# A graph layer on one core: keys packed once for all edges, a reordered preparation, and the test for further passes moved

## The chip, the core and the metric

One core of a Trainium2 chip runs the whole program. The time is the device time of one execution, in microseconds. An execution of the kernel before took 666.23 us (median of 3 runs, 665.59 to 668.93). The engines are TensorE (PE in the rows; PEld is its weight load), VectorE (DVE), ScalarE (ACT), GpSimd (POOL) and SyncE (SP, which only issues DMAs here). An engine works its instructions off in program order, and waits on semaphores hold up all that is behind them.

## The reference

6250 nodes of 96 values, 206250 edges sorted by their target `dst`, and a small perceptron:

```python
h = maximum(layernorm(x), 0)
m = h[src] + edge_attr                       # 206250 x 96
aggr = segment_sum(m, dst, num_segments=6250)
hidden = relu(aggr @ W1 + b1)                # 96 -> 192
out = x + (1 + eps) * h + hidden @ W2 + b2   # 192 -> 96
```

## The kernel before

The nodes are cut into 49 blocks of 128. Since `dst` is sorted, the edges of a block lie together. For each block the kernel builds, without any gather, an adjacency count: for every node of the block how often each of the 6250 sources points at it. Aggregation is then `adj` (counts) times `h`, plus the sums of the edge rows.

Preparation, once. `dst` is loaded as 127 rows of 1632 (`D`), every 32nd of its values is taken as a sample, and one-hots of the samples and 51 matmuls give the histogram from which the start row of each node in the sorted list follows (`hist`, `total`, `cnt`, `row`). GpSimd subtracts neighbours in `D` (line 369) and VectorE takes the minimum (`falls`), to see whether `dst` is sorted. `row` gives the place of each node's window of 128 edges (`row_i`) and, spread by matmul, the edge row at which each group of 32 nodes starts (`e_tab`), which SyncE reads for its loads. Beside it VectorE and ScalarE make `h` (mean, centre, square, variance, root, scale; lines 499 to 516) and split it in two fp16 parts `hl` (lines 518 to 522). Copies of `src` and `dst` with a padded tail are written to DRAM, since the windows are fetched from there.

The loop over blocks b = 0 to 48 (and one more turn of TensorE and ScalarE). All engines work on different blocks at the same time, ordered by semaphores:

- GpSimd, once for two blocks (a pair): two indirect DMAs fetch the windows of 128 edges of 128 target pairs from the padded `src` and `dst`; ten vector instructions of 128 columns compute a low key (source modulo 128) and a high key (source block and which of the two targets) from them (`keys`, lines 373 to 391); then it adds the bias `b2` to the pair's part of `x_sb`.
- TensorE turns a pair's keys (`turn_keys`, line 814). ScalarE copies the turned keys out of PSUM, each value twice, once per block (`next_keys`, 256 columns, behind its octet copy 6).
- VectorE compares: `hot` (which of 32 nodes an edge belongs to, from the block's 4 x 10 x 128 edge ids), and in four chunks the one-hots `z` (source block) and `lo_hot` (source modulo 128) (line 494).
- TensorE multiplies `lo_hot` and `z` in eight octets of 8 slots, into one of two PSUM banks in turn; ScalarE copies each octet to `adj` (line 722). TensorE sums the edge rows (80 passes of 32 columns, behind octet 3), one block later the slots `adj` x `hl` (49 matmuls, line 832, behind octet 1), then turns the sums (line 837, behind octet 4), and runs the perceptron. ScalarE takes the low half of the sums, the turned sums and the relu from PSUM; VectorE joins (line 618) and adds the result to `x_sb` (line 625).
- SyncE loads the edge rows and ids of each block in four groups (`load`, lines 291 to 296), into a ring of 4 buffers (`TURN`), and stores block b - 8 behind the load of block b. The residual `x + (1 + eps) h` (line 589) stands on VectorE between block 0 and block 1. `h` lives in buffers 2 and 3 of the edge ring, so loads 2 and 3 wait for the residual.

The end. A window may be too short for unusual inputs; the number of passes that is needed is computed on VectorE (`passes_needed`, behind the last block) and each engine tests it: if it is over 1 (it is 1 here) a general loop would do all again. Before the test, all five engines wait for all stores (`all_stored`).

Of the kernel before, what the change touches and what calls it, by code (L numbers as in the profile page):

```python
# [12 lines left out]
P = 128  # L13
# [10 lines left out]
TURN = 4  # L24
SCALE = 4096.0
EDGES_AFTER = 3
ROUND = 12582912.0


def build(nc, x, src, dst, edge, w1, b1, w2, b2, eps, out):  # L30
# [3 lines left out]
    NT = -(-N // P)  # L34
    NLAST = N - (NT - 1) * P
    ZW = NT * TILE_NODES
    SAMPLES = -(-E // STEP)
    PAIRS = -(-NT // 2)
    GE = P * GT
    ELAST = E - GE  # L40
    GCOLS = PAIRS * 2 * GROUPS
    TURNS = NT // TURN
    assert NT == TURNS * TURN + 1 and ZW % 2 == 0

# [4 lines left out]
    assert 0 < DREST < DW and DW % STEP == 0  # L49

    EVEN = E // 16 * 16
    PADDED = (SAMPLES + 4) * STEP
    PAD = PADDED - EVEN
# [3 lines left out]
    FAR = 32767  # L57

    with ExitStack() as ctx:
# [8 lines left out]

        src_pad = nc.dram_tensor("src_padded", [PADDED], I32).ap()
        dst_pad = nc.dram_tensor("dst_padded", [PADDED], I32).ap()  # L70
        src_rows = src_pad.rearrange("(r k) -> r k", k=STEP)
        dst_rows = dst_pad.rearrange("(r k) -> r k", k=STEP)
# [7 lines left out]
        dst_sb = [sb(f"dst{k}", [P, GROUPS, GT], I32) for k in range(TURN)]  # L80
        z_home = sb("z", [P, CHUNKS, CHUNK, ZW], F16)
# [3 lines left out]
        hot = [sb(f"hot{k}", [P, GROUPS * GT, GROUP]) for k in range(2)]  # L85
        rel = [sb(f"rel{k}", [P, GROUPS, GT]) for k in range(2)]
        key2 = [sb(f"key{k}", [P, 2, TPB, 2], F16) for k in range(2)]

        win_src = [sb(f"win_src{k}", [P, P], I32) for k in range(2)]
        win_dst = [sb(f"win_dst{k}", [P, P], I32) for k in range(2)]  # L90
        k_lo = sb("k_lo", [P, P])
        k_hi = sb("k_hi", [P, P])
        k_a = sb("k_a", [P, P])
        k_src = sb("k_src", [P, P])
        k_w = sb("k_w", [P, P])
        keyT = [sb(f"keyT{k}", [P, 2, P]) for k in range(2)]
# [15 lines left out]
        total = sb("total", [PAIRS, P])  # L112
# [8 lines left out]
        picked = sb("picked", [P, 2, PAIRS, 2 * GROUPS])  # L121
# [25 lines left out]
        tail_ids = sb("tail_ids", [1, 2, PAD], I32)  # L147
# [10 lines left out]
        ob = [sb(f"ob{k}", [P, C]) for k in range(TURN)]  # L158
# [790 lines left out]
```

## Time and profile before

| | before |
|---|---|
| median of 3 runs | 666.23 us |
| the profiled execution's own time | 665.97 us |
| its span, first to last instruction | 664.1 us |
| VectorE busy | 586.3 us, 88% |
| TensorE busy | 536.5 us, 81% |
| GpSimd busy | 473.9 us, 71% |
| ScalarE busy | 374.3 us, 56% |
| DMA moved | 109.72 MB, 165 GB/s on average |

Busy times are sums over the whole span. No engine is busy throughout, and the chain from one block to the next runs over several engines; so the table alone doesn't tell what sets the time. The granted clock of TensorE is 1.00 of its 2.4 GHz from 50 to 640 us.

### The profile page before, as it was taken

Reading aid. Unit: us, or ns where it says so; the run is one execution under the profiler, and the core shown is the slowest. Engines: PE = TensorE matmul, PEld = TensorE weight load, DVE = VectorE, ACT = ScalarE, POOL = GpSimd, SP = SyncE. Lnnn points to the kernel's source line nnn. Section 1 sums busy time; section 2 is a strip of 40 time slices with the busy share of each in tenths; the row PEclk is TensorE's granted clock in tenths of the full one; section 3 lists DMA queues with packets and bytes.
Section 4 is the critical chain, followed back from the end, with each engine's and each line's share of the span. In section 5 each row is a group of like instructions: output and inputs, shape, how many; then the busy total and the mean of one; then the engine's idle time right before and its main releaser. Section 6 shows DMA issues by size and latency. Waiting matters only on the chain. (4 is left out here: it accounts for less than half of the span.)

```text
span 664.1 us, 24207 instructions
## 1 busy us (share of the span) xinstructions
PE 536.5 (81%) x10016; PEld 492.7 (74%) x10016; DVE 586.3 (88%) x649; ACT 374.3 (56%) x645; POOL 473.9 (71%) x393
## 2 busy tenths in 40 slices
PE   0301598999989999898998989999899998989982
PEld 0301487888878888788888878888788887888881
DVE  6998699999999999999999999999999999999830
ACT  2221356567565665756667565665656657566650
POOL 4199999999977977977887797797779777730000
PEclk9999999999999999999999999999999999999997
DMA  8271785656656565565646656465564665644000
GB/s 244 66 223 38 239 259 154 189 170 193 192 165 201 152 205 182 162 195 174 206 159 184 188 172 204 156 189 191 164 198 158 197 187 171 200 139 125 6 5 9
DMA packets 67888, 109.72 MB, mean 165 GB/s; under 512 B 40093, under 2 KB 41727, under 8 KB 67742
## 3 DMA queue, kind: packets, MB, share of 16 engines
q1 hardware_dynamic: 66174, 104.84, 51.9%
q0 software_dynamic: 1600, 3.28, 1.6%
q8 instruction: 81, 1.33, 0.8%
q14 instruction: 33, 0.27, 0.1%
HBM read 105.69 MB, written 4.05 MB: 165 GB/s over the span
## 5 line engine op out<-in xcount | busy, mean ns | idle before, releaser
L722 ACT ACTIVATE adj<-oct_ps 128x784 f16<-128x784 f32 x392 | 316.8, 872 | 79.1 <-PE oct_ps L820 73.8
L494 DVE TENSOR_TENSOR lo_hot<-iota_z,key 128x2048 f16<-128x2048 f16 x196 | 263.9, 1346 | 0.0
L820 PE MATMUL oct_ps<-z,lo_hot 128*128 128x98 f16 x3136 | 201.1, 208 | 48.7 <-ACT adj L722 39.6
L494 DVE TENSOR_TENSOR z<-iota_z,key 128x1568 f16<-128x1568 f16 x196 | 198.5, 1013 | 36.2 <-PE oct_ps L820 35.5
L820 PEld LDWEIGHTS oct_ps<-z,lo_hot 128*128 128x128 f16 x3136 | 162.3, 98 | 78.7 <-issue 54.8
L832 PE MATMUL agg_ps<-hl,adj 128*128 128x192 f16 x2401 | 206.0, 246 | 0.0
L832 PEld LDWEIGHTS agg_ps<-hl,adj 128*128 128x128 f16 x2401 | 196.9, 98 | 0.2 <-ACT adj L722 0.2
L728 ACT ACTIVATE low<-agg_ps 128x96 f32<-128x96 f32 x49 | 12.3, 252 | 157.3 <-PE agg_ps L832 157.3
L826 PE MATMUL agg_ps<-edges,hot 128*32 128x96 f32 x3920 | 92.6, 250 | 0.0
L826 PEld LDWEIGHTS agg_ps<-edges,hot 128*32 128x32 f32 x3920 | 81.9, 111 | 4.1
L598 DVE TENSOR_TENSOR hot<-iota_w,rel 128x1280 f32<-128x1280 f32 x49 | 73.6, 1502 | 1.7
L375 POOL TENSOR_SCALAR k_hi<-win_src 128x128 f32<-128x128 int32 x25 | 18.4, 738 | 65.4 <-PE key_ps L814 64.9
L394 POOL DMA_INDIRECT win_src<-src_padded,row_i x25 | 43.6, 1743 | 18.3 <-DVE row_i L549 14.3
L396 POOL DMA_INDIRECT win_dst<-dst_padded,row_i x25 | 39.2, 1567 | 7.6 <-issue 7.6
L846 PE MATMUL mlp_ps<-w_sb,hid 96*128 96x96 f32 x196 | 33.6, 294 | 8.4 <-ACT hid L735 6.0
L385 POOL TENSOR_SCALAR k_lo<-k_hi 128x128 f32<-128x128 f32 x25 | 38.4, 1537 | 2.1
L377 POOL TENSOR_SCALAR k_a<-win_dst,base 128x128 f32<-128x128 int32 x25 | 37.7, 1507 | 0.0
L846 PEld LDWEIGHTS mlp_ps<-w_sb,hid 96*128 96x128 f32 x196 | 25.5, 190 | 15.8 <-ACT hid L735 15.8
L383 POOL TENSOR_SCALAR k_w<-k_w 128x128 f32<-128x128 f32 x25 | 35.1, 1403 | 1.6
L814 PE MATMUL key_ps<-ident,keyT 128*128 128x128 f32 x50 | 10.5, 294 | 31.5 <-POOL keyT L391 31.5
L388 POOL TENSOR_TENSOR keyT<-k_lo,k_src 128x128 f32<-128x128 f32 x25 | 33.0, 1322 | 2.0
L419 POOL TENSOR_TENSOR x_sb<-x_sb,b_sb 128x192 f32<-128x192 f32 (+1 forms) x25 | 33.8, 1353 | 0.0
(110 smaller groups left out, 452.8 us busy)
## 6 DMA issues: line engine op xcount, KB each, us to landing
edges<-in_edge_attr SPq DMA_DIRECT2D x196, 480.0 KB, 4.6
dst<-in_dst SPq DMA_DIRECT2D x196, 5.0 KB, 3.5
out<-ob SPq DMA_DIRECT2D x48, 48.0 KB, 4.3
src_padded<-in_src SPq DMA_DIRECT2D x1, 805.6 KB
dst_padded<-in_dst SPq DMA_DIRECT2D x1, 805.6 KB
edges<-in_dst SPq DMA_DIRECT2D x1, 803.7 KB
win_src<-src_padded,row_i POOLq DMA_INDIRECT x25, 5.2
win_dst<-dst_padded,row_i POOLq DMA_INDIRECT x25, 5.2
```

The lines of the kernel that those rows point to most:

```text
L377: nc.gpsimd.tensor_scalar(k_a[:, :], wd, column, None, ALU.subtract).then_inc(done, 1)
L383: nc.gpsimd.tensor_scalar(k_w[:, :], k_w[:, :], 512.0, 127.5, ALU.mult, ALU.subtract).then_inc(done, 1)
L385: nc.gpsimd.tensor_scalar(k_lo[:, :], k_hi[:, :], -float(P // 2), None, ALU.mult)
L394: nc.gpsimd.indirect_dma_start(out=ws, out_offset=None, in_=src_rows, in_offset=bass.IndirectOffsetOnAxis(ap=index, axis=0)).then_inc(done ...
L396: nc.gpsimd.indirect_dma_start(out=wd, out_offset=None, in_=dst_rows, in_offset=bass.IndirectOffsetOnAxis(ap=index, axis=0)).then_inc(done ...
L494: return nc.vector.tensor_tensor(out.rearrange("p t (w two) -> p t w two", two=2), iota_z[0:out.shape[0], 0:width].rearrange("p (o w two) ...
L598: return nc.vector.tensor_tensor(hot[buf][:, :, :], iota_w[:, :].rearrange("p (o w) -> p o w", o=1).broadcast_to([P, GROUPS * GT, GROUP]), ...
L722: return nc.scalar.activation(adj[k][:, :, 2 * OCT * o:2 * OCT * (o + 1)].rearrange("p h (t q) -> p t h q", q=2), oct_ps[:, o % 2, :].rear ...
L820: last = nc.tensor.matmul(oct_ps[:, o % 2, P * t:P * t + ZW], lo_hot[o // 2][:, at, :], z[o // 2][:, at, :], start=True, stop=True)
L826: last = nc.tensor.matmul(agg_ps[buf][GROUP * g:GROUP * (g + 1), 0:C], hot[buf][:, g * GT + t, :], edges[k][:, g, t, :], start=fresh and t ...
L832: last = nc.tensor.matmul(agg_ps[buf][:, 0:2 * C], adj[buf][:, h, :], hl[:, h, :], start=False, stop=(h == NT - 1), skip_group_check=True)
L846: last = nc.tensor.matmul(mlp_ps[:, 3 * P:3 * P + C], hid[:, j, :], w2_sb[:, j, :], start=(j == 0), stop=(j == H - 1))
```

## The change

- **Keys packed once.** In the preparation all edges are turned into two words: `64 * dst + (src >> 7)` as an integer, and `src & 127` as a float (two vector passes over `src`, one that joins `D`, one ScalarE copy; 1632 columns each). One DMA writes them, 1.67 MB, to DRAM. A window is one indirect DMA of both words, with three windows in flight. Of the key arithmetic one VectorE instruction per pair is left (`pick`: subtract the pair's base, divide by 64); `z` is compared with marks t/64 + j, for source block t and target j of a tile of two. GpSimd has no vector work in the loop. The padded copies in DRAM go.
- **Key copies.** ScalarE copies a pair's keys in one instruction of 512 columns, behind octet copy 3 of every even block, in place of one of 256 columns behind octet copy 6 of every block.
- **Preparation reordered.** `dst` and `src` are loaded before `x`. GpSimd's neighbour differences wait for the sample one-hots. Mean and variance come from `bn_stats`, one instruction per tile of 128 nodes; ScalarE makes `h` with a relu with bias and scale per tile (49 instructions of 96 columns), in two halves, before it copies the first keys. The low parts of `hl` move from ahead of block 0 to between block 0 and 1, in front of the residual.
- **Bias.** `b2` is added to all of `x_sb` by one GpSimd instruction of 4704 columns once `h` is complete, and the residual waits for it.
- **Buffers.** The edge ring has 3 buffers. `h` lies in 1 and 2 of them, so loads 1 and 2 wait for the residual. Stores lag by 6 blocks, with 4 output buffers as before.
- **Test for further passes.** Only SyncE waits for all stores ahead of the test; the other engines do it at the end of their own work, and wait for the stores inside the branch.
- Code for blocks whose source rows would be gathered (`GATHERED`) is added and is off: all 49 blocks are counted as before.

The diff, cut:

```diff
-TURN = 4
+TURN = 3
+OBS = 4
+WINS = 3
...
+            sp.wait_ge(words_ready, 1)
+            sp.wait_ge(lows_ready, 1)
+            sp.dma_start(keys_dram.rearrange("(p k) e -> p (k e)", p=P), packed.rearrange("p e two -> p (e two)")).then_inc(keys_stored, 16)
...
             sp.wait_ge(tab_ready, 1)
             load(0)
-            load(1)
+            sp.wait_ge(h_ready, 2)
             sp.wait_ge(res_ready, 1)
+            load(1)
             load(2)
-            load(3)
...
             pool.wait_ge(row_ready, 1)
-            pool.wait_ge(pads_in, 64)
-            fetch(0)
-            pair(0)
+            pool.wait_ge(keys_stored, 16)
+            for q in range(WINS):
+                fetch(q)
             pool.wait_ge(w_in, 16 * 5)
             nc.gpsimd.tensor_scalar(eps_sb[:, :], eps_sb[:, :], 1.0, None, ALU.add).then_inc(eps_ready, 1)
+            pool.wait_ge(h_ready, 2)
+            nc.gpsimd.tensor_tensor(x_sb[:, :, :], x_sb[:, :, :],
+                                    b2_sb[:, :].rearrange("p (o c) -> p o c", o=1).broadcast_to([P, NT, C]), ALU.add).then_inc(bias_added, 1)
...
+                for t in range(ROWS[k].start, ROWS[k].stop):
+                    last = nc.scalar.activation(h_sb[:, t, :], x_sb[:, t, :], ACT.Relu, bias=shift[:, t:t + 1], scale=rstd[:, t:t + 1])
+                last.then_inc(h_ready, 1)
...
-                    if o == 6 and b + 2 < NT:
-                        next_keys(b + 2)
+                    if o == 3 and b % 2 == 0 and b // 2 + 1 < MPAIRS:
+                        next_keys(b // 2 + 1)
...
             for b in range(NM):
                 if b == 1:
+                    low_part(0)
+                    low_part(1)
                     residual()
...
-            all_stored(act)
...
             with act.If(passes > 1):
+                all_stored(act)
```

The order of instructions shows the two places on which most depends. First VectorE, from the end of the preparation over block 0 to block 1 (`hl` are the low parts, `keyT` is the pick, `rel` and `hot` open a block, `z` and `lo_hot` are a chunk). Before:

```order
L521 SCALAR_TENSOR_TENSOR hl<-edges,hl 128x24x96
L521 SCALAR_TENSOR_TENSOR hl<-edges,hl 128x25x96
L592 TENSOR_TENSOR rel<-dst,gbase 128x40
L598 TENSOR_TENSOR hot<-iota_w,rel 128x1280
L494 TENSOR_TENSOR z<-iota_z,key 128x1568
L494 TENSOR_TENSOR lo_hot<-iota_z,key 128x2048
...
L494 TENSOR_TENSOR lo_hot<-iota_z,key 128x2048
L589 SCALAR_TENSOR_TENSOR x_sb<-edges,eps_sb,x_sb 128x4704
L592 TENSOR_TENSOR rel<-dst,gbase 128x40
L598 TENSOR_TENSOR hot<-iota_w,rel 128x1280
```

After:

```order
L545 SCALAR_TENSOR_TENSOR shift<-stat,rstd 128x25
L635 TENSOR_TENSOR rel<-dst,gbase 128x40
L641 TENSOR_TENSOR hot<-iota_w,rel 128x1280
L521 TENSOR_TENSOR z<-z_marks,key 128x1568
L521 TENSOR_TENSOR lo_hot<-iota_z,key 128x2048
L604 TENSOR_SCALAR keyT<-win,base 128x128
...
L521 TENSOR_TENSOR lo_hot<-iota_z,key 128x2048
L551 SCALAR_TENSOR_TENSOR hl<-edges,hl 128x24x96
L551 SCALAR_TENSOR_TENSOR hl<-edges,hl 128x25x96
L632 SCALAR_TENSOR_TENSOR x_sb<-edges,eps_sb,x_sb 128x4704
L635 TENSOR_TENSOR rel<-dst,gbase 128x40
L641 TENSOR_TENSOR hot<-iota_w,rel 128x1280
```

The two low parts stood ahead of block 0 and now stand behind it, next to the residual; a pick, for the pair after, is new within block 0.

Second ScalarE, behind the slot sums of block 0 and into block 2 (`adj` an octet copy, `key` the key copy, `hid` the relu). Before:

```order
L728 ACTIVATE low<-agg_ps 128x96
L722 ACTIVATE adj<-oct_ps 128x8x49x2 x3
L731 ACTIVATE aggT<-mlp_ps 96x128
L722 ACTIVATE adj<-oct_ps 128x8x49x2 x2
L710 ACTIVATE key<-key_ps 128x256
L735 ACTIVATE hid<-mlp_ps,b_sb 96x128 x2
L722 ACTIVATE adj<-oct_ps 128x8x49x2 x3
```

After:

```order
L807 ACTIVATE hid<-mlp_ps,b_sb 96x128 x2
L791 ACTIVATE adj<-oct_ps 128x8x49x2 x3
L797 ACTIVATE low<-agg_ps 128x96
L791 ACTIVATE adj<-oct_ps 128x8x49x2 x2
L779 ACTIVATE key<-key_ps 128x512
L791 ACTIVATE adj<-oct_ps 128x8x49x2
L803 ACTIVATE aggT<-mlp_ps 96x128
L791 ACTIVATE adj<-oct_ps 128x8x49x2 x2
L807 ACTIVATE hid<-mlp_ps,b_sb 96x128 x2
```

The key copy has left its place in front of the relu; a wider one stands behind octet copy 3 of the even block.

Third GpSimd, which before repeated this for every pair:

```order
L394 DMA win_src<-src_padded,row_i 128x128
L396 DMA win_dst<-dst_padded,row_i 128x128
L375 TENSOR_SCALAR k_hi<-win_src 128x128
...
L389 TENSOR_TENSOR k_w<-k_w,k_hi 128x128
L391 TENSOR_SCALAR keyT<-k_w 128x128
L419 TENSOR_TENSOR x_sb<-x_sb,b_sb 128x192
```

After, all that it does from the first window on:

```order
L425 DMA win<-packed_keys,row_i 128x256 x3
L438 TENSOR_SCALAR eps_sb<-eps_sb 128x1
L440 TENSOR_TENSOR x_sb<-x_sb,b_sb 128x4704
L425 DMA win<-packed_keys,row_i 128x256 x22
L460 MEMSET zeros 128x128
```

Of the vector work one add over all nodes is left, between the third window and the fourth.

## Rows read from the trace of the kernel before

**Rows 1.** Waits of the whole span: engine, line, whom it waited for, us, times, longest.

```profile
PE oct_ps L820 <- ACT adj L722: 39.6, 93, 0.7
```

**Rows 2.** Timeline of TensorE, line 837: start us, us, engine, line, op, tiles, [idle before].

```profile
89.14 0.28 PE L837 MATMUL mlp_ps<-ident,agg 128*96 128x128 f32 x1
...
312.61 0.27 PE L837 MATMUL mlp_ps<-ident,agg 128*96 128x128 f32 x1
...
324.25 0.28 PE L837 MATMUL mlp_ps<-ident,agg 128*96 128x128 f32 x1
...
629.82 0.27 PE L837 MATMUL mlp_ps<-ident,agg 128*96 128x128 f32 x1
...
641.18 0.27 PE L837 MATMUL mlp_ps<-ident,agg 128*96 128x128 f32 x1
...
650.21 0.29 PE L837 MATMUL mlp_ps<-ident,agg 128*96 128x128 f32 x1 [0.89 <-DVE ob L625]
```

**Rows 3.** Busy time by window: us, then each engine's busy us, clock, DMA share, GB/s.

```profile
600.00:640.00 40.00, 37.02 (x715) 34.56 (x716) 32.81 (x49) 23.71 (x42) 0.00 (x0) 1.00 0.13 44
```

**Rows 4.** Timeline of ScalarE in the middle of the loop.

```profile
303.29 0.39 ACT L710 ACTIVATE key<-key_ps 128x256 f16<-128x256 f32 x1
...
303.55 0.65 ACT L735 ACTIVATE hid<-mlp_ps,b_sb 96x128 f32<-96x128 f32 x2
...
312.81 0.84 ACT L722 ACTIVATE adj<-oct_ps 128x784 f16<-128x784 f32 x1 [1.19 <-PE oct_ps L820]
```

**Rows 5.** TensorE's last matmuls, in its timeline.

```profile
652.25 0.69 PE L846 MATMUL mlp_ps<-w_sb,hid 96*128 96x96 f32 x4 [0.71 <-ACT hid L735]
```

**Rows 6.** Sequencer instructions of lines 926 and 59: duration ns min/median/max, first to last start.

```profile
L926 PEldq COMPARE_BRANCH  x1: 3967/3967/3967, 656.5 to 656.5; - x1
...
L59 SPq DRAIN  x1: 53/53/53, 656.9 to 656.9; - x1
...
L59 POOLq DRAIN  x1: 4224/4224/4224, 659.6 to 659.6; - x1
```

**Rows 7.** Timeline of VectorE in the preparation.

```profile
8.21 2.55 DVE L501 TENSOR_REDUCE stat<-x_sb 128x24 f32<-128x2304 f32 x1 [4.82 <-DMA x_sb<-in_x]
...
13.49 2.90 DVE L527 TENSOR_SCALAR s_v<-edges 127x51 int32<-127x51 int32 x1
...
17.04 3.56 DVE L494 TENSOR_TENSOR lo_hot<-iota_z,s_key 127x6528 f16<-127x6528 f16 x1
...
21.28 1.85 DVE L536 TENSOR_REDUCE falls<-edges 127x1 f32<-127x1632 int32 x1
...
43.87 5.47 DVE L521 SCALAR_TENSOR_TENSOR hl<-edges,hl 128x2304 f16<-128x2304 f32 x2
...
51.93 0.20 DVE L592 TENSOR_TENSOR rel<-dst,gbase 128x40 f32<-128x40 int32 x1 [2.60 <-ACT key L710]
...
62.24 5.14 DVE L589 SCALAR_TENSOR_TENSOR x_sb<-edges,eps_sb,x_sb 128x4704 f32<-128x4704 f32 x1
```

**Rows 8.** Timeline of GpSimd in the preparation.

```profile
11.47 4.86 POOL L369 TENSOR_TENSOR edges<-edges 127x1632 int32<-127x1632 int32 x1 [8.42 <-DMA edges<-in_dst]
...
71.74 0.45 POOL L389 TENSOR_TENSOR k_w<-k_w,k_hi 128x128 f32<-128x128 f32 x1
...
72.78 0.58 POOL L419 TENSOR_TENSOR x_sb<-x_sb,b_sb 128x192 f32<-128x192 f32 x1
```

**Rows 9.** Groups by shape: count, busy us, mean ns, idle before.

```profile
L419 POOL TENSOR_TENSOR x_sb<-x_sb,b_sb 128x192 f32<-128x192 f32 x24 | 32.5, 1352 | 0.0
...
L598 DVE TENSOR_TENSOR hot<-iota_w,rel 128x1280 f32<-128x1280 f32 x49 | 73.6, 1502 | 1.7
...
L625 DVE TENSOR_TENSOR ob<-x_sb,mlp_ps 128x96 f32<-128x96 f32 x49 | 11.9, 242 | 3.0 <-issue 3.0
```

**Rows 10.** Timeline of SyncE, the last id DMA of load 2.

```profile
72.89 0.33 SPq L295 DMA_DIRECT2D dst<-in_dst  x1
```

**Rows 11.** DMA issues of the page: count, KB each, us to landing.

```profile
dst<-in_dst SPq DMA_DIRECT2D x196, 5.0 KB, 3.5
```

More of the change, by code:

```diff
@@ L41, in build @@
     GCOLS = PAIRS * 2 * GROUPS
-    TURNS = NT // TURN
-    assert NT == TURNS * TURN + 1 and ZW % 2 == 0
+    assert ZW % 2 == 0 and NT <= SPREAD and len(ATTACHED) == GATHERED and not any(a % 2 for a in ATTACHED)
     DP = 126
@@ L487, in _, with one_hots @@
             nc.vector.tensor_scalar(ident[:, :], diff_i[:, :], 0.0, None, ALU.is_equal)
-            nc.vector.tensor_scalar(below[:, :], diff_i[:, :], 0.0, None, ALU.is_gt)
-            nc.vector.tensor_scalar(upto[:, :], diff_i[:, :], 0.0, None, ALU.is_ge).then_inc(consts, 1)
+            nc.vector.tensor_scalar(below, diff_i[:, :], 0.0, None, ALU.is_gt)
+            nc.vector.tensor_scalar(upto, diff_i[:, :], 0.0, None, ALU.is_ge).then_inc(consts, 1)
             v.wait_ge(consts, 1)
             v.wait_ge(bases_ready, 1)
-            def one_hots(out, keys, tiles, width):
+            def one_hots(out, keys, marks, tiles, width):
@@ L494, in one_hots @@
                 return nc.vector.tensor_tensor(
                     out.rearrange("p t (w two) -> p t w two", two=2),
-                    iota_z[0:out.shape[0], 0:width].rearrange("p (o w two) -> p o w two", o=1, two=2).broadcast_to([out.shape[0], tiles, width // 2, 2]),
+                    marks[0:out.shape[0], 0:width].rearrange("p (o w two) -> p o w two", o=1, two=2).broadcast_to([out.shape[0], tiles, width // 2, 2]),
                     keys.rearrange("p t (o two) -> p t o two", o=1).broadcast_to([out.shape[0], tiles, width // 2, 2]), ALU.is_equal)
-            def mean(k):
-                v.wait_ge(x_in[k], 16 * (k + 1))
-                chain(nc.vector.tensor_reduce(stat[:, ROWS[k]], x_sb[:, ROWS[k], :], AX_X, ALU.add))
-                chain(nc.vector.tensor_scalar(stat[:, ROWS[k]], stat[:, ROWS[k]], 1.0 / C, None, ALU.mult))
@@ new lines, in variance @@
+            def variance(k):
+                sl = ROWS[k]
+                parts = [bn[:, sl, c:c + 1].rearrange("p t o -> p (t o)") for c in range(6)]
+                both, apart, spread = (stat[:, c, sl] for c in range(3))
+                nc.vector.tensor_tensor(both, parts[1], parts[4], ALU.add)
+                nc.vector.tensor_tensor(spread, parts[2], parts[5], ALU.add)
+                chain(nc.vector.tensor_tensor(apart, parts[1], parts[4], ALU.subtract))
+                chain(nc.vector.tensor_tensor(apart, apart, apart, ALU.mult))
+                chain(nc.vector.scalar_tensor_tensor(spread, apart, C / 4.0, spread, ALU.mult, ALU.add))
+                nc.vector.tensor_scalar(spread, spread, 1.0 / C, 1e-5, ALU.mult, ALU.add).then_inc(var_ready, 1)
@@ L634, in _ @@
                     join(b - 2)
+                if attached(b - 2) is not None:
+                    finish_gathered(attached(b - 2))
+                if b % 2 == 0 and b // 2 + 1 < MPAIRS:
+                    pick(b // 2 + 1)
                 for c in range(1, CHUNKS):
@@ L747, in _ @@
                         read_octet(b % 2, o).then_inc(oct_read, 1)
+                    if o == 0 and behind is not None:
+                        act.wait_ge(gather_aggT_done, behind + 1)
+                        take_turned(gather_aggT, key_ps).then_inc(gather_aggT_ready, 1)
                     if o == 1 and b >= 1:
```

526 lines of the change are left out of this document (300 added, 226 removed).

## The prediction

> **What bounds the kernel now.** I read the waits first: TensorE's largest repeated wait in the loop is for ScalarE to read an octet bank, 39.6 us in 93 pieces [rows 1]; VectorE has the highest busy share of the page, but in the loop it waits for TensorE. So the second view is the pace: the moment in each block at which TensorE turns the sums (line 837), 89.14 in block 1 and 650.21 in block 49, 561.1 us for 48 steps, 11.69 each; a step without key transposes is 11.64 (312.61 to 324.25) [rows 2]. Third, does GpSimd's key arithmetic cost the loop anything? It has nothing to do between 600 and 640 us [rows 3], and there the step keeps its length until block 47. So the 10 vector instructions per pair that leave GpSimd are worth nothing in the loop, although VectorE's and GpSimd's instructions delay each other.
>
> What then makes the step? ScalarE's queue in the second half of a block: octet copy, turned sums, two octet copies, key copy, relu, octet copies; the key copy at 303.29 and relu at 303.55 stand in it back to back [rows 4], and TensorE may fill an octet bank only when it has been read. Blocks 47 and 48 have no key copy left: from 629.82 to 641.18 the step is 11.36 against 11.64 [rows 2]. That is the price of one key copy in this place, 0.28 us, and it agrees with its pitch before relu (303.29 to 303.55, 0.26) [rows 4].
>
> **Loop.** The change makes one copy of 512 columns for a pair instead of two of 256, and puts it behind octet copy 3 of even blocks. From 0.39 us for 256 columns and 0.84 for 784 (0.85 ns a column) it takes some 0.61, pitch 0.5; ScalarE idles 1.19 us there before the next octet copy [rows 4], so it is covered; without cover it would cost at most 25 x 0.5 = 12 us. Key copies of blocks 1 to 46 leave the path: 46 x 0.27 = 12.4 us (0.27 lies between the two readings). VectorE gets one pick per pair, a 128-column instruction of some 0.2 us; it loses the delays by GpSimd and stays behind TensorE's pace. The ring of three edge buffers lets a load start 3 blocks ahead, 35 us for four groups that need 5.5 us to issue and 3.5 to land (the load of block 1 below): nothing. DMA carries as many edge bytes as before. So the loop from block 1 to 49 takes 561.1 - 12.4 = 548.7.
>
> **End.** TensorE's last projection starts at 652.25 and takes 0.69 [rows 5]. The test for further passes then stood on all engines behind the last store; TensorE's jump over the unused code took 3.97 us, and GpSimd's DRAIN, the last thing of all, began at 659.6 and took 4.22 [rows 6]. Now GpSimd tests as soon as the flag exists (long before), and TensorE right behind its last matmul: 652.9, 0.9 for load and register work, 3.97, so 657.9; SP, which still waits for the stores, had its DRAIN at 656.9 [rows 6]. End at 658.1 instead of 664.1: 6.0 us less (5 to 7, by whether the jump costs its 3.97 again).
>
> **Start.** The whole question is when block 1 can turn its sums; before at 89.14. I follow the new order.
> - dst lands. Half of x, 1.18 MB and issued first, landed at 8.21; dst alone was there at 11.47, behind x [rows 7, 8]. Now dst (0.80 MB) goes first but waits for its memset until 2.6: 8.5 (7.5 to 11.5).
> - Sample one-hots: four small instructions 0.8, then 3.56 [rows 7] and by columns 0.7: 13.5.
> - Two passes of 1632 columns over src (1.85 each by the reduction of the same width [rows 7]), and GpSimd's difference pass beside them. Here a small instruction is telling: s_v, 51 columns, took 2.90 us, until GpSimd's instruction over 1632 columns ended [rows 7, 8]. VectorE can be held by GpSimd for a whole instruction; I add 1.0 for that: 18.2 (16.5 to 20).
> - Word pass 1.85, the minimum 1.85, small copies 0.6: 22.5. 12 BN_STATS: the trace has none; 96 columns are 0.11 us by the reduction's rate and 0.24 by the 96-column add of line 625 [rows 7, 9]; I take 0.17, 49 are 8.3 us (5.4 to 11.9). 24.5; the row chain, ten small instructions at some 0.2 (rel took 0.20 [rows 7]): 26.6; 12 more, variance, table, shift, 5.1: 31.7.
> - ScalarE makes h in 49 instructions of 96 columns. Nearest row: two relu of 128 columns with bias in 0.65 [rows 4]; so 0.25 each by pitch (0.2 to 0.33). 24 tiles 6.0, high part 2.1 (0.85 ns a column), square root and shift 0.9, 25 tiles 6.3: h complete at 47.0 (43 to 53). Keys of block 0 are copied at 49.8 (before 51.93, when VectorE started [rows 7]).
> - But at 47.0 GpSimd starts the bias add over all of x_sb, 4704 columns in one instruction. By 0.45 us for 128 and 0.58 for 192 columns [rows 8] it is 2.03 ns a column: 9.7 us. Bounds: 4.86 us for 1632 columns gives 14.0; the 2.90 in which s_v was held gives 8.4. It starts first, VectorE is idle, and VectorE's next instruction reads two SBUF tensors: I take it to be held until 56.8.
> - Block 0: 9.9, pick among it (before 10.3: 51.93 to 62.24 [rows 7], hots 1.5 of it [rows 9], so a chunk is 2.1 and some 2.03 undisturbed); low parts 5.5 and residual 5.1 [rows 7], both now between block 0 and 1: 77.3.
> - Load 1 waits for the residual (before, it was issued at once, and only load 2 waited). The last id DMA of such a load went out 5.5 us behind the residual's end (67.38 to 72.89), 3.5 to land [rows 10, 11]: ids at 86.3. Then hots 1.6, first chunk 2.0, three chunks 6.1, hots of block 2 1.6, its chunk 2.0, join 0.2: TensorE turns the first sums at 100, and some 0.5 for its own late start: 100.5. That is 11.4 us later than before (2 to 24 later).
>
> The stall that goes is TensorE's in block 0 for the keys of the second pair, now picked on VectorE; what is late next is the ids of block 1.
>
> **Rules weighed.** The rows show s_v held until GpSimd's end. The Trainium skill, "SBUF — State Buffer", Who interferes with whom, says the same more strongly: the shared port pair is locked for the whole instruction, and a VectorE instruction with two SBUF inputs meets a GpSimd one that reads SBUF. By that rule the long add keeps VectorE off for all its length; without it the sum would be 7 us smaller (the first rival). For the add's price the rows give 9.7 us; the Trainium skill, "GPSIMD Engine Reference", Reconciling with measured numbers, has 4497 ns for 2048 fp32 elements, by which I estimate 10.3 us, and the sum would be 0.6 more.
>
> **Sum.** 664.1 + 11.4 - 12.4 - 6.0 = 657.1 us of span. The profiled execution took 665.97 for 664.1, and the median is 666.23: 659.1 in time.
>
> **Rivals.**
> - *The long add does not hold VectorE.* Block 0 then starts at 49.8 instead of 56.8 and the residual finds bias and low parts ready: 7 us less, 652. For it: on GpSimd many short adds ran beside VectorE's; against it: s_v.
> - *The loop gives nothing.* If another wait fills the place of the key copy, 12.4 come back: 671.5. Against it speaks the step of 11.36 at the end.
> - *Slower by the start: the bias add at GpSimd's price in the loop.* Its mean there is 1352 ns for 192 columns [rows 9], 7.0 ns a column, 33.1 us if that were its own rate, 23.4 more: 682. Place: between h complete and block 0. With 16.8 us of add the time is that of before, from 20.2 it is slower by 0.5%. Against it: 0.58 us with VectorE idle.
> - *Preparation dearer.* 0.36 per ScalarE tile and 0.24 per BN_STATS: 5.4 and some 2 more, 666: no change.
> - *The change does not do what it says:* the end keeps its 6 us because GpSimd's DRAIN waits for something else; 665.
>
> **Numbers.** Forecast (654 to 663.5 of its own) 0.54; add not holding 0.16; loop gives nothing 0.08; add dear 0.06; preparation dear 0.12; end kept 0.04. Under 662.9 is faster by over 0.5%, above 669.6 slower by as much, which is about what a measurement of this kernel can tell from no change. Faster: 0.16 and most of 0.54, 0.66. Slower: 0.08, 0.06 and a rest of the preparation, 0.15. Range 650 to 669.
>
> **What would show it.** The steps between TensorE's turnings of the sums: 11.37 and 11.6 in turn (right), 11.64 and 11.87 (wrong). GpSimd's one add of 4704 columns: 9.7 us, and VectorE's rel of block 0 starting or ending with it. Residual's end 77, first id DMA of load 1 behind it, first turned sums 100.5. GpSimd's DRAIN well before 650, last DRAIN of all on TensorE near 658 less the shift. If block 1 turns its sums later than 107.6, the forecast's sign is wrong.

## The result: slower by 0.8%, and the profile after

| | before | after |
|---|---|---|
| median of 5 runs each, on one chip | 666.61 us | 672.13 us (671.05 to 672.97) |
| span of the profiled execution | 664.1 us | 671.1 us |
| first turned sums (line 918, was 837), block 1 | 89.14 | 105.19 |
| last turned sums, block 49 | 650.21 | 663.66 |
| loop between them | 561.07 | 558.47 |
| from there to the end | 13.9 | 7.4 |

The ratio is 1.0078, 95% interval 1.0055 to 1.0101: slower, where 659.1 us was forecast. The time lies outside the range. The span is the sum +16.05 -2.6 -6.4 = +7.0 against the forecast's +11.4 -12.4 -6.0 = -7.0. The end came as worked out, the start 4.7 us worse, and 9.8 us of the loop's gain are not there.

**The loop.** TensorE's timeline after: edge sums (L907) and turned sums (L918) of blocks 2 to 4 and of three of the last turns. Columns as in [rows 2].

```profile
114.66 2.33 PE L907 MATMUL agg_ps<-edges,hot 128*32 128x96 f32 x80
117.29 0.27 PE L918 MATMUL mlp_ps<-ident,agg 128*96 128x128 f32 x1
126.50 1.86 PE L907 MATMUL agg_ps<-edges,hot 128*32 128x96 f32 x80
128.66 0.27 PE L918 MATMUL mlp_ps<-ident,agg 128*96 128x128 f32 x1
138.11 2.35 PE L907 MATMUL agg_ps<-edges,hot 128*32 128x96 f32 x80
140.76 0.27 PE L918 MATMUL mlp_ps<-ident,agg 128*96 128x128 f32 x1
...
629.72 1.86 PE L907 MATMUL agg_ps<-edges,hot 128*32 128x96 f32 x80
631.88 0.27 PE L918 MATMUL mlp_ps<-ident,agg 128*96 128x128 f32 x1
...
654.63 0.27 PE L918 MATMUL mlp_ps<-ident,agg 128*96 128x128 f32 x1
663.66 0.28 PE L918 MATMUL mlp_ps<-ident,agg 128*96 128x128 f32 x1 [0.88 <-DVE ob L668]
```

The step to an odd block is 11.37 (117.29 to 128.66), as forecast. The step to an even block is 12.10 (128.66 to 140.76) where 11.6 was forecast, and there the same 80 edge matmuls take 2.35 instead of 1.86. From block 42 on all edge sums take 1.86. What else happens in those 2.35 us? The timeline of all engines in block 4, same columns:

```profile
137.54 0.28 PE L896 MATMUL key_ps<-ident,win 128*128 128x128 f32 x1
...
138.09 0.95 POOL L425 DMA_INDIRECT win<-packed_keys,row_i  x1 [22.30 <-PE key_ps L896]
138.11 0.96 PEld L907 LDWEIGHTS agg_ps<-edges,hot 128*32 128x32 f32 x42
138.11 2.35 PE L907 MATMUL agg_ps<-edges,hot 128*32 128x96 f32 x80
...
139.12 0.60 ACT L779 ACTIVATE key<-key_ps 128x512 f16<-128x512 f32 x1
139.40 0.84 PEld L907 LDWEIGHTS agg_ps<-edges,hot 128*32 128x32 f32 x38 [0.32 <-issue]
```

TensorE's weight loads stop once, from 139.07 to 139.40, with no semaphore to wait for ("issue"). GpSimd's window fetch ends at 139.04. The key copy starts at 139.12. It is no wait for instructions to be loaded either: between 138.0 and 140.5 the DMA view lists no packet of an instruction queue, and the loads go on at 139.40 without one. Twenty such pauses stand in the trace, one in each even block from 2 to 40, and the last window fetch of the program is the one in block 40 (560.29); key copies go on to block 46. In block 2 the fetch takes longer:

```profile
114.64 1.16 POOL L425 DMA_INDIRECT win<-packed_keys,row_i  x1 [37.28 <-PE key_ps L896]
```

It ends at 115.80, while the pause stands where it does in the other blocks, from 115.62 to 115.94. So the pause lies close to the end of the fetch, but doesn't follow it exactly. Twenty times 0.47 us is 9.4: the forecast's 548.7 for the loop with it is 558.1, and 558.47 was measured.

**The start.** ScalarE's timeline after, in the preparation:

```profile
30.84 8.70 ACT L773 ACTIVATE edges<-x_sb,shift,rstd 128x96 f32<-128x96 f32 x24 [1.32 <-issue]
...
42.41 9.05 ACT L773 ACTIVATE edges<-x_sb,shift,rstd 128x96 f32<-128x96 f32 x25 [0.60 <-DVE shift L545]
51.49 2.20 ACT L776 ACTIVATE hl<-edges 128x2400 f16<-128x2400 f32 x1
53.60 0.58 ACT L779 ACTIVATE key<-key_ps 128x512 f16<-128x512 f32 x1
```

GpSimd's, which answers to [rows 8]:

```profile
51.54 10.10 POOL L440 TENSOR_TENSOR x_sb<-x_sb,b_sb 128x4704 f32<-128x4704 f32 x1 [20.75 <-ACT edges L773]
61.79 2.35 POOL L425 DMA_INDIRECT win<-packed_keys,row_i  x1 [0.15 <-issue]
69.08 8.28 POOL L425 DMA_INDIRECT win<-packed_keys,row_i  x1 [4.94 <-PE key_ps L896]
```

And VectorE's, which answers to [rows 7]:

```profile
22.06 2.00 DVE L528 BATCH_NORM_STATS2 hot<-x_sb 128x6 f32<-128x96 f32 x12
...
30.62 0.18 DVE L545 SCALAR_TENSOR_TENSOR shift<-stat,rstd 128x24 f32<-128x24 f32 x1
...
54.21 7.48 DVE L635 TENSOR_TENSOR rel<-dst,gbase 128x40 f32<-128x40 int32 x1 [11.84 <-ACT key L779]
...
71.42 5.12 DVE L551 SCALAR_TENSOR_TENSOR hl<-edges,hl 128x2304 f16<-128x2304 f32 x2
76.45 5.11 DVE L632 SCALAR_TENSOR_TENSOR x_sb<-edges,eps_sb,x_sb 128x4704 f32<-128x4704 f32 x1
91.27 0.20 DVE L635 TENSOR_TENSOR rel<-dst,gbase 128x40 f32<-128x40 int32 x1 [9.71 <-DMA dst<-in_dst]
```

The shift is there at 30.8, 0.9 earlier than forecast. The 49 ScalarE tiles then take 17.75 us, 0.36 each, and h is complete at 51.5 instead of 47.0. From there everything is as worked out, later by that: `rel` of 40 columns, which took 0.20 before [rows 7], lasts from 54.21 to 61.69 and ends with GpSimd's add at 61.64; the residual ends at 81.56; and VectorE has nothing to do for 9.71 us until the ids of block 1 are in.

TensorE meanwhile idles from 76 to 95. Windows of the span, columns as in [rows 3]:

```profile
75.00:90.00 15.00, 0.48 (x8) 0.33 (x8) 6.56 (x2) 1.45 (x2) 2.36 (x1) 0.65 0.36 109
90.00:95.00 5.00, 0.00 (x0) 0.00 (x0) 3.69 (x5) 0.00 (x0) 0.00 (x0) 0.50 0.91 306
95.00:105.00 10.00, 9.93 (x165) 9.49 (x166) 9.97 (x13) 3.51 (x5) 0.00 (x0) 0.75 0.88 296
```

After that idle time the granted clock is at its lower level (0.50 of 2.4, so 1.2 GHz) and comes back near 100 us. The slot sums of block 1 took 6.01 us, in part at that level. But VectorE sets the first turned sums: from `rel` at 91.27 to the join of block 1 at 104.65 its instructions follow one another without a wait, 13.38 us, and e4 below, with 10 us less of that idle time, has the same 13.38 (80.78 to 94.16). From the join to the turned sums it is 0.54, so up to there the lower clock can have cost no more than that.

**The end.** Sequencer instructions of lines 1030 and 68 after; columns as in [rows 6].

```profile
L1030 PEldq COMPARE_BRANCH  x1: 3624/3624/3624, 666.8 to 666.8; - x1
```

```profile
L68 POOLq DRAIN  x1: 2178/2178/2178, 654.2 to 654.2; - x1
...
L68 PEldq DRAIN  x1: 73/73/73, 670.4 to 670.4; - x1
L68 SPq DRAIN  x1: 43/43/43, 670.8 to 670.8; - x1
```

GpSimd is done at 656.4, and the last turned sums to the end are 7.4 us instead of 13.9.

### The profile page after: what moved, and what is told of

Its sections match the earlier page's. It is cut to its first block, busy times and chain, and to the rows that moved or that the text cites. A ratio compares the mean times of both kernels' runs of the same rounds, so it can differ in the third digit from the quotient of the medians.

```text
span 671.1 us, 23925 instructions
## 1 busy us (share of the span) xinstructions
PE 540.1 (80%) x10016; PEld 497.8 (74%) x10016; DVE 558.5 (83%) x730; ACT 387.9 (58%) x669; POOL 49.2 (7%) x43
## 4 chain that ended last, share of the span: by engine, by line
PE 58%; ACT 30%; DVE 8%; issue 2%; SPq 1%; DMA 1%; DVEq 0%; ACTq 0%
PE agg_ps L913 30%; ACT adj L791 22%; PE agg_ps L907 14%; PE oct_ps L901 13%; ACT hid L807 3%; ACT edges L773 3%; DVE lo_hot L521 2%; DVE rel L635 1%; ACT aggT L803 1%; DVE z L521 1%; DMA gathered_edges<-in_dst 1%; DVE x_sb L632 1%; DVE hl L551 1%; ACT hl L776 1%; DVE hot L528 1%
## 5 line engine op out<-in xcount | busy, mean ns | idle before, releaser
L521 DVE TENSOR_TENSOR lo_hot<-iota_z,key 128x2048 f16<-128x2048 f16 x196 | 238.6, 1217 | 0.0
L521 DVE TENSOR_TENSOR z<-z_marks,key 128x1568 f16<-128x1568 f16 x196 | 190.3, 971 | 47.1 <-PE oct_ps L901 45.7
L907 PE MATMUL agg_ps<-edges,hot 128*32 128x96 f32 x3920 | 99.9, 250 | 2.1 <-issue 0.3
L907 PEld LDWEIGHTS agg_ps<-edges,hot 128*32 128x32 f32 x3920 | 85.1, 111 | 10.3 <-issue 6.3
L425 POOL DMA_INDIRECT win<-packed_keys,row_i x25 | 32.9, 1315 | 480.1 <-PE key_ps L896 469.7
L635 DVE TENSOR_TENSOR rel<-dst,gbase 128x40 f32<-128x40 int32 x49 | 16.7, 340 | 21.6 <-ACT key L779 11.8
L662 DVE TENSOR_TENSOR agg<-agg_ps,low 128x96 f32<-128x96 f32 x49 | 12.6, 258 | 23.7 <-ACT low L797 23.7
L922 PE MATMUL mlp_ps<-aggT,w_sb 96*96 96x128 f32 x196 | 31.4, 283 | 0.4 <-ACT aggT L803 0.4
L807 ACT ACTIVATE hid<-mlp_ps,b_sb 96x128 f32<-96x128 f32 x98 | 30.8, 381 | 0.8 <-PE mlp_ps L922 0.8
L922 PEld LDWEIGHTS mlp_ps<-aggT,w_sb 96*96 96x96 f32 x196 | 22.8, 163 | 0.6 <-ACT aggT L803 0.6
L773 ACT ACTIVATE edges<-x_sb,shift,rstd 128x96 f32<-128x96 f32 x49 | 17.8, 452 | 1.9 <-issue 1.3
L779 ACT ACTIVATE key<-key_ps 128x512 f16<-128x512 f32 x25 | 15.0, 598 | 0.0
```

Of the source, the lines that this page charges most:

```text
L425: nc.gpsimd.indirect_dma_start(out=to[:, :, :].rearrange("p e two -> p (e two)"), out_offset=None, in_=keys_dram, in_offset=bass.IndirectO ...
L521: return nc.vector.tensor_tensor(out.rearrange("p t (w two) -> p t w two", two=2), marks[0:out.shape[0], 0:width].rearrange("p (o w two) - ...
L635: nc.vector.tensor_tensor(rel[buf][:, :, :], ids[:, :, :], gbase[:, at].rearrange("p (g o) -> p g o", o=1).broadcast_to([P, GROUPS, GT]), ...
L773: last = nc.scalar.activation(h_sb[:, t, :], x_sb[:, t, :], ACT.Relu, bias=shift[:, t:t + 1], scale=rstd[:, t:t + 1])
L807: last = nc.scalar.activation(to[:, j, :], bank[0:C, P * (1 + j):P * (2 + j)], ACT.Relu, bias=b1_sb[:, j:j + 1])
L907: last = nc.tensor.matmul(sums[GROUP * g:GROUP * (g + 1), :], hots[:, g * GT + t, :], rows[:, g, t, :], start=fresh and t == 0, stop=False ...
```

## The experiments

Two theories on the pause. **A**: GpSimd's window fetch causes it; in a wide form wherever matmuls run beside it, in a narrow form only within the edge sums. **B**: ScalarE's key copy of 512 columns, which begins there, causes it. All runs were timed in three rounds beside the kernel before, e1 to e4 on one chip and e5 to e12 on another, so ratios compare better than times; the ratio is to the kernel before. "First" is the first turned sums, "loop" from there to the last, "end" the rest, each read from one profiled execution. "First" varies by some 0.9 us either way without a cause in the edit: after, e1, e2, e3, e5 and e12 share their preparation and lie between 103.8 and 105.5.

| | us | ratio (95%) | first | loop | end |
|---|---|---|---|---|---|
| after | 672.13 | 1.0078 (1.0055 to 1.0101) | 105.2 | 558.5 | 7.4 |
| e1 fetch behind edge sums | 662.53 | 0.9934 (0.9911 to 0.9957) | 104.9 | 548.5 | 7.4 |
| e2 fetch in slot sums | 662.33 | 0.9927 (0.9907 to 0.9946) | 104.2 | 548.8 | 7.4 |
| e5 memset in its place | 662.80 | 0.9950 (0.9932 to 0.9967) | 105.5 | 548.7 | 7.4 |
| e12 fetch shifted | 665.40 | 0.9984 (0.9974 to 0.9994) | 104.7 | 551.0 | 7.0 |
| e3 key copy behind octet 6 | 682.89 | 1.0239 (1.0217 to 1.0261) | 103.8 | 568.2 | 7.1 |
| e4 h elsewhere | 661.74 | 0.9923 (0.9900 to 0.9945) | 94.5 | 557.5 | 7.5 |
| e8 bias by pair, on e1 | 654.84 | 0.9839 (0.9815 to 0.9864) | 97.5 | 548.2 | 7.5 |
| e6 before, late tests | 657.95 | 0.9883 (0.9862 to 0.9904) | 88.3 | 560.7 | 7.1 |
| e7 before, key copy by pair | 650.50 | 0.9772 (0.9751 to 0.9793) | 86.4 | 548.3 | 13.6 |
| e11 before, both | 645.99 | 0.9690 (0.9673 to 0.9706) | 87.7 | 549.6 | 7.1 |
| e9 = e1 + e4 + e8 | 646.84 | 0.9705 (0.9689 to 0.9722) | 89.1 | 548.3 | 7.5 |
| e10 = e9, h shared | 634.79 | 0.9523 (0.9508 to 0.9539) | 77.0 | 548.8 | 7.4 |

**e1: the fetch waits for the edge sums.**

```diff
             def fetch(q):
                 if q >= WINS:
                     pool.wait_ge(turned, q - WINS + 1)
+                if q >= WINS + 1:
+                    pool.wait_ge(edges_done, 2 * q - 7)
```

> The changed kernel, with each window fetch of GpSimd waiting also for the edge sums of the block, so that its indirect DMA no longer runs beside them. In the changed kernel the edge sums of even blocks 2 to 40 take 0.47 us longer than those of odd ones (steps 12.09 and 11.37), and not from block 42 on, when the fetches are over. Theory A (the pause belongs to the indirect DMA that ends within the edge sums): the 20 pauses go, even steps 11.62, 9.4 us less than the changed kernel. Theory B (the pause belongs to the wide key copy of ScalarE, which starts at the same moment): even steps stay at 12.09, 0 us. Theory C (a slowdown of the edge sums by something of the even blocks that neither of them makes): 0 us.

Steps 11.61 and 11.36 in turn, loop 548.5. In block 4 of its timeline the edge sums are whole and the fetch stands behind them:

```profile
137.09 1.86 PE L909 MATMUL agg_ps<-edges,hot 128*32 128x96 f32 x80
...
139.74 0.95 POOL L425 DMA_INDIRECT win<-packed_keys,row_i  x1 [21.81 <-PE agg_ps L909]
```

The whole missing gain of the loop comes back with one wait on an engine that is idle for 93% of the time. That is Theory A, and neither B nor C: the copy stands where it stood, 1.02 us behind the start of the edge sums.

**e2: the same, into the slot sums.** The wait is `pool.wait_ge(oct_done, (2 * q - 7) * OCTS + 2)` instead.

> The changed kernel, with each window fetch held until octet 1 of the next block is done, so that its indirect DMA runs and ends within the slot sums, 4.2 us in which TensorE has no slack. Theory A in its wide form (TensorE pauses wherever such a DMA ends): a pause of 0.35 to 0.47 us moves into the slot sums, and the time stays that of the changed kernel. Theory A in its narrow form (only beside the edge sums of 32 columns in fp32, or only together with the key copy): no pause, even steps 11.62, 9.4 us less.

Loop 548.8 and no pause, though the fetch, now 2.15 us long, ends beside running slot sums of 128-column fp16 matmuls. The wide form of A falls, with one reserve: here the fetch is also twice as long, and no run put a fetch of 0.95 us beside such matmuls.

**e3: the key copy behind octet copy 6** (`o == 3` becomes `o == 6` ahead of `next_keys`).

> The changed kernel, with the wide key copy behind octet copy 6 of the even blocks instead of octet copy 3; the fetches stay where they are. If the pause needs only the indirect DMA: the edge sums of even blocks keep their 2.08 us between first and last start, and the copy adds its pitch of some 0.5 us to 23 steps, so 11 us more than the changed kernel. If the pause needs the key copy (alone or together with the DMA): the edge sums go to 1.61, which takes back 9.4 us, and the time is within 2 us of the changed kernel.

The timeline of its block 4:

```profile
136.31 0.95 POOL L425 DMA_INDIRECT win<-packed_keys,row_i  x1 [21.66 <-PE key_ps L896]
136.32 2.33 PE L907 MATMUL agg_ps<-edges,hot 128*32 128x96 f32 x80
...
141.49 0.62 ACT L779 ACTIVATE key<-key_ps 128x512 f16<-128x512 f32 x1
```

The pause is there with the copy 4 us away: Theory B falls. And the copy in this place lengthens each of 23 steps to an odd block from 11.37 to 11.84, by 0.47, near the pitch of 0.5 that the forecast worked out for it from [rows 4]. The loop is only 568.2 - 558.5 = 9.8 us longer, because its first step is 11.23 for 12.10: in block 2 the fetch took 1.80, ended behind the last weight load, and nothing paused.

**e5: a memset of the fetch's length in the fetch's place**, the fetch itself behind the edge sums.

```diff
...
+                    nc.gpsimd.memset(scratch[0][:, 0:1100], 0).then_inc(busy_done, 1)
+                    pool.wait_ge(edges_done, 2 * q - 7)
```

> As the kernel whose fetches wait for the edge sums (660.8 us of span), but in the old place of each fetch GpSimd now runs a memset of 1100 columns into an unused buffer, some 1 us, so that another GpSimd instruction runs and ends within the edge sums of the even blocks from 2 on. If any GpSimd instruction that ends there makes TensorE pause: even steps 12.09 again, 9 to 10 us more than that kernel. If it takes the indirect DMA: even steps stay 11.61, and the time stays within 1.5 us of it.

```profile
137.71 1.01 POOL L436 MEMSET gathered_edges<- 128x1100 int32 x1 [19.63 <-PE key_ps L903]
137.94 1.64 PEld L914 LDWEIGHTS agg_ps<-edges,hot 128*32 128x32 f32 x80
```

The memset ends at 138.72, inside the edge sums, and all 80 weight loads run in one piece. A memset reads nothing; but in the kernel before GpSimd's key arithmetic, which reads, stands beside these sums too (122.30 to 123.97 beside those of 122.35), and they take 1.86. It takes the indirect DMA, not just any GpSimd work.

**e12: the fetch 0.5 us later**, behind a memset of 400 columns, to see whether the pause follows its end.

> The changed kernel, with a GpSimd memset of 400 columns, some 0.45 us, ahead of each window fetch, so that the indirect DMA ends 1.4 instead of 0.93 us after the edge sums' start. If the pause belongs to the moment at which the indirect DMA ends: it stays 0.35 us long and moves to 1.4 us behind the start of the edge sums, and the time stays within 1 us of the changed kernel. If it belongs to a moment of TensorE's or ScalarE's own work, and the DMA only makes it possible: it stays at 0.93, or goes.

It met neither expectation:

```profile
137.12 1.75 PEld L913 LDWEIGHTS agg_ps<-edges,hot 128*32 128x32 f32 x80
137.12 1.96 PE L913 MATMUL agg_ps<-edges,hot 128*32 128x96 f32 x80
137.47 1.55 POOL L426 DMA_INDIRECT win<-packed_keys,row_i  x1 [0.15 <-POOL gathered_edges L436]
```

Started beside a running VectorE instruction, the fetch took 1.55 instead of 0.95 and ended with the edge sums; the sums lost only 0.1, in each even block from 4 to 40. In block 2 alone the fetch (114.12 to 115.55) ended earlier against the sums, and there the weight loads stop for 0.25, from 115.39 to 115.64, 0.67 later within the sums than in block 2 of the changed kernel. So the run did not put the end of the fetch where it was meant to be, and what exactly in a fetch stops TensorE stays open.

**e7: the kernel before, with only the key copy by pair** (as in the change: one copy of 512 columns behind octet copy 3 of even blocks).

```diff
-                    if o == 6 and b + 2 < NT:
-                        next_keys(b + 2)
+                    if o == 3 and b % 2 == 0 and b // 2 + 1 < PAIRS:
+                        next_keys(b // 2 + 1)
```

> The kernel before, with only the key copies changed: one of 512 columns for a pair, behind octet copy 3 of the even blocks. The prediction's term for the loop: 46 x 0.27, 12.4 us less, steps 11.37 and 11.6, if GpSimd's indirect DMAs (two per pair, slowed by VectorE) don't end within the edge sums. If they do, or the pause is the copy's: even steps 12.1, 3 us less or none. Rival: GpSimd's chain of 12 instructions per pair (19.9 us of 23.5) becomes the pace: steps stay above 11.6.

Loop 548.3, 12.8 less than before where the forecast's term was 12.4. Its GpSimd does all the key arithmetic still. In five blocks of the loop (2, 5, 7, 10, 12) a fetch of its ends within the edge sums, as here in block 7:

```profile
152.72 1.61 POOL L396 DMA_INDIRECT win_dst<-dst_padded,row_i  x1 [0.30 <-issue]
153.10 1.64 PEld L826 LDWEIGHTS agg_ps<-edges,hot 128*32 128x32 f32 x80
```

The fetch ends at 154.33 and nothing pauses, nor in the other four. It differs from the changed kernel's in two ways: windows of 512 bytes a row instead of 1024, and 1.61 us instead of 0.95 beside VectorE. Neither was tried alone. From block 13 on no fetch of e7 touches edge sums at all, and in the kernel before none from block 9 on: there GpSimd comes to its fetches behind the key arithmetic, 4.4 and 6.6 us after the start of the edge sums of an odd block. In the trace of before:

```profile
416.09 1.86 PE L826 MATMUL agg_ps<-edges,hot 128*32 128x96 f32 x80
...
420.52 1.84 POOL L394 DMA_INDIRECT win_src<-src_padded,row_i  x1 [0.16 <-issue]
...
422.67 1.61 POOL L396 DMA_INDIRECT win_dst<-dst_padded,row_i  x1 [0.30 <-issue]
```

So for most of the loop the place of the fetches alone keeps TensorE free.

**e4: h in the unused gather buffers**, so that load 1 follows load 0 at once.

```diff
-        h_sb = edge_home[:, 1:3, :, :, :].rearrange("p k g t c -> p (k g t c)")[:, 0:NT * C].rearrange("p (t c) -> p t c", c=C)
+        h_sb = gather_home[:, :, :, :, :].rearrange("p k g t c -> p (k g t c)")[:, 0:NT * C].rearrange("p (t c) -> p t c", c=C)
...
-            sp.wait_ge(h_ready, 2)
-            sp.wait_ge(res_ready, 1)
             load(1)
```

> The changed kernel, with h in the two buffers that serve as scratch in the preparation, so that the loads of blocks 1 and 2 are issued right behind load 0 and wait for nothing. My account of the start (VectorE stands 9.71 us between the residual and the ids of block 1): the first sums are turned 9.5 us earlier, at 95.7 instead of 105.2, and the whole is 9 to 10 us shorter. Rival (the DMAs of three blocks beside the preparation delay the window fetches and x): the preparation gets longer by more than 3 us and the gain is under 6.

First sums at 94.5, 10.7 earlier than after: 9.7 for the wait, 0.7 by which its block 0 happened to start earlier (53.51 for 54.21), and 0.2 behind the join (0.31 for 0.54). VectorE's timeline of it goes from the residual into block 1 without the 9.71 us:

```profile
75.75 5.12 DVE L630 SCALAR_TENSOR_TENSOR x_sb<-gathered_edges,eps_sb,x_sb 128x4704 f32<-128x4704 f32 x1
80.78 0.20 DVE L633 TENSOR_TENSOR rel<-dst,gbase 128x40 f32<-128x40 int32 x1
```

**e8: on e1, the bias added pair by pair behind the residual**, as before the change, instead of in one instruction.

```diff
-            pool.wait_ge(h_ready, 2)
-            nc.gpsimd.tensor_tensor(x_sb[:, :, :], x_sb[:, :, :],
...
+            pool.wait_ge(res_ready, 1)
+            for q in range(WINS):
+                add_bias(q)
...
```

> As the kernel whose fetches wait for the edge sums, but with the bias added pair by pair by GpSimd behind the residual, as before the change, in place of one add of 4704 columns. By the lock theory (VectorE's first instruction of block 0 took 7.49 us because the add of 10.1 us held it): that instruction takes 0.2 us, the residual ends 7.3 us earlier, and the first sums are turned some 7.3 us earlier, at 97.6; the loop keeps 548.5, since VectorE has slack for being delayed by 24 short adds. Rival (VectorE waited for its ids or something else): no gain.

```profile
53.98 0.20 DVE L644 TENSOR_TENSOR rel<-dst,gbase 128x40 f32<-128x40 int32 x1 [11.84 <-ACT key L789]
```

`rel` takes 0.20 again, and the first sums come 7.4 us earlier than in e1. The loop pays nothing for the 25 short adds.

**e6, e11: the kernel before with the late tests**, alone and with the key copy by pair.

```diff
-            all_stored(pool)
...
             with pool.If(passes > 1):
+                all_stored(pool)
```

(the same for the other three engines but SyncE)

> The kernel before, with only the wait for all stores moved from ahead of the test for further passes into its branch, on all engines but SyncE. By my account of the end (13.9 us from the last turned sums to the end before, 7.4 in the changed kernel): 6.4 us less, 657.7 of span, nothing else moved. Rival (GpSimd's DRAIN waits for something else that now comes late): under 3 us less.

> The kernel before with two parts of the change alone: the late test and the wide key copy. The two measured alone were 8.0 and 15.8 us of span; if they add up, span 664.1 - 23.8 = 640.3, and by the terms of the rows (loop 548.3, end 7.1, first sums between 86.4 and 89.1) 641.8 to 644.5. Rival (the wider copy brings GpSimd's chain to the pace): over 646.

e6: the end falls from 13.9 to 7.1. e11: loop 549.6, end 7.1, span 644.3, within its range. Two small edits of the change, without its preparation, packing or buffers, are 3.1% faster than before. But e11 has the 512-byte rows of e7, and its edge sums are 0.14 to 0.21 us longer in the four blocks of the loop in which a fetch ends within them (3, 5, 8, 10). In block 5:

```profile
131.37 1.61 POOL L396 DMA_INDIRECT win_dst<-dst_padded,row_i  x1 [0.30 <-issue]
...
131.75 1.79 PEld L826 LDWEIGHTS agg_ps<-edges,hot 128*32 128x32 f32 x80
```

The fetch stands to the sums as in block 7 of e7, where the weight loads took 1.64. What tells the two apart is open; rows of 512 bytes don't rule the pause out.

**e9, e10: the changed kernel mended.** e9 has the edits of e1, e4 and e8. e10 also gives half of h back to VectorE, in two instructions of 2400 columns, and puts ScalarE's first key copy ahead of the high parts.

```diff
+            chain(nc.vector.scalar_tensor_tensor(h_sb[:, HALF:NT, :], wide(stat[:, 0, HALF:NT]), -0.5, x_sb[:, HALF:NT, :], ALU.mult, ALU.add))
...
+            nc.vector.scalar_tensor_tensor(h_sb[:, HALF:NT, :], h_sb[:, HALF:NT, :], 0.0, wide(rstd[:, HALF:NT]), ALU.max, ALU.mult).then_inc(h_ready, 1)
```

> The three repairs together on the changed kernel: fetches behind the edge sums, bias pair by pair, h in the scratch buffers so that loads 1 and 2 wait for nothing. If the losses add up: first sums turned at 97.5 - 9.8 = 87.7, loop 548.3, end 7.5, span 643.5, which is 27.6 less than the changed kernel and 20.6 less than before. Rival (with the ids early, another wait opens between block 0 and 1, such as the window of pair 1 or GpSimd's adds): first sums later than 90.

> As the three repairs, and ScalarE makes only the first 24 tiles of h one by one (0.36 us each); the other 25 are made by VectorE in two instructions of 2400 columns, where it was idle, and the first key copy stands ahead of the two high-part copies. By the prediction's corrected start (the 49 ScalarE instructions are the chain up to block 0): block 0 starts on VectorE at 41.7 instead of 54, first sums turned at 75.4, span 631. Rival (block 0 is then held by its window, its ids or the turned keys): first sums at 80 or later.

The first sums came 1.4 and 1.6 us later than expected; in e10's block 1 VectorE's instructions are longer beside GpSimd's three adds (`hot` 1.88 instead of 1.49). VectorE's timeline of e10:

```profile
36.01 2.65 DVE L624 SCALAR_TENSOR_TENSOR gathered_edges<-stat,x_sb 128x2400 f32<-128x2400 f32 x1
...
41.62 0.19 DVE L651 TENSOR_TENSOR rel<-dst,gbase 128x40 f32<-128x40 int32 x1
```

Block 0 starts at 41.6, where it started at 51.9 before [rows 7] and at 54.2, held until 61.7, after. e10 takes 634.79 us: 4.8% less than before, 5.5% less than after (0.9523 / 1.0078 = 0.945).

## Why the prediction was wrong

- **Loop, expected -12.4, got -2.6.** The step as put ("Key copies of blocks 1 to 46 leave the path: 46 x 0.27 = 12.4 us") held: e7 gives -12.8. What failed is the step by which the 10 vector instructions per pair that leave GpSimd are worth nothing in the loop: it asked for their own time and left out where the fetches behind them would go, a term of +9.8 us. Before, the fetches stood in a busy queue, and from block 9 on all of them came behind the edge sums. With an empty queue each fetch now starts as soon as TensorE has transposed the window (138.09, behind 137.54), and that is where TensorE's edge sums begin. Twenty pauses of 0.47 us are 9.4, and e1, which moves only the fetches, gets 10.0 back. The rival "loop gives nothing" came near in size, by luck: its reason, another wait in the place of the key copy, is false by e1 and e7. That the fetch in this place makes the pause is shown by e1, e3 and e5 (e2 agrees); the mechanism below it is not.
- **Start, expected +11.4, got +16.0.** The mis-sized term is ScalarE's tile: 0.25 taken, 0.36 measured, 49 x 0.11 = 5.4, less the 0.9 by which the shift was early. My nearest row was a relu with a bias alone [rows 4]; this one also has a scale per partition. 0.36 was the price in "preparation dearer", whose other part was not true: BN_STATS took 0.17, as taken. The Trainium skill, "ScalarE: Activation LUTs", What ACT_TABLE_LOAD costs, gives 186 ns and 0.833 ns a column, 93 ns for each operand that is a per-partition pointer, and an overlap of 93 ns back to back. By that I estimate 452 ns for one such tile and 359 by pitch. The trace has a mean of 452 ns and a pitch of 362: it agrees, and had the page been weighed for this instruction, the term would have been right.
- **The long add** took 10.10 us for 4704 columns, 9.7 taken, and held VectorE for 7.48. e8 takes the lock away and gets 7.4 us: the rival "does not hold VectorE" is false, and the rule of the Trainium skill ("SBUF — State Buffer", Who interferes with whom) that the prediction names is borne out. The rival "the bias add at GpSimd's price in the loop", 7.0 ns a column, is false as well (2.15).
- **The wait for the ids of block 1** was worked out as 9.0 us (77.3 to 86.3) and took 9.7. e4, without it, has the first sums 10.7 earlier, 0.7 of it from its earlier block 0.
- **End, expected -6.0, got -6.4.** Right, by the right rows; e6 alone gives -6.8. Only the last DRAIN of all is SyncE's, 0.4 behind TensorE's.
- **The sign.** The warning in the prediction was block 1 later than 107.6. It came at 105.2, and alone would have left a gain of 2.7 us: 664.1 + 16.05 - 12.4 - 6.4 = 661.4. The pauses turned the sign. A chance of 0.08 for a loop without gain was too small: a change that empties a queue moves every transfer that the queue had delayed, and I asked what the freed time was worth, not where the fetches would land.

## What to carry to other kernels

When work leaves an engine, follow what is left in its queue to its new place in time, transfers above all, and ask what stands there; the cure may be one more wait on the idle engine. An instruction over a whole tensor on GpSimd can be one long lock for VectorE (7.5 us here), and short ones behind the critical piece cost next to nothing (e8; in e9 and e10 some 1.5 us of block 1). A buffer that is lent to another tensor makes a load wait: price the DMA issue and landing behind its release before the ring is made smaller.

## What the runs showed of the hardware

- An indirect DMA of GpSimd (128 rows of 1 KB, 0.95 us on GpSimd) that runs with the first half of a series of 80 fp32 matmuls of 32 stationary columns stops TensorE's weight loads for 0.28 to 0.34 us, and lengthens the series by 0.44 to 0.49 (after, e3, e4). Not so a fetch of 2.15 us beside fp16 matmuls of 128 columns (e2), nor a memset of 1.01 us (e5). Fetches of 512-byte rows that ended within the series lengthened it by nothing in e7 (five blocks) and by 0.14 to 0.21 in e11 (four). The Trainium skill, "SBUF — State Buffer", Who interferes with whom, has it that TensorE never waits for anyone at SBUF's ports. The trace shows a stop that no semaphore explains; whether a port has to do with it no run shows.
- The same indirect DMA takes 0.95 us where nothing on VectorE was running when it began, 1.55 in e12, 2.15 in e2, and 8.28 beside the last one-hots of block 0, VectorE's two passes over `h` and the start of a third (69.08 to 77.36). So it takes longer beside VectorE's instructions; only in e12 did an edit bring that about, and there by accident. Not every VectorE instruction does it to the same degree: the first window's fetch, begun beside BN_STATS, took 1.15 (26.80 to 27.95).
- An ACTIVATE of 96 columns with bias and scale per partition: 452 ns, pitch 0.36 us; BN_STATS of 96 columns: pitch 0.17 us.
- TensorE's jump over the unused branch takes 3.4 to 4.0 us over all runs; GpSimd's DRAIN takes 4.2 in the kernel before and 2.2 in the changed one. In e6 the DRAIN is over at 643.5, and the jump (652.1 to 655.7) runs while SyncE waits for the last stores until 655.3: beside that wait both cost next to nothing.
